# A transformer block on one core: the projections issued as 32-column matmuls behind the weighted sums

## What is computed

```python
x = x + _L0_attn_a_ref(_layernorm(x, axis=-1), ...)
x = x + _L0_ffn_ref(_layernorm(x, axis=-1), ...)
x = x + _L0_attn_b_ref(_layernorm(x, axis=-1), ...)
x = x + _L0_ffn_ref(_layernorm(x, axis=-1), ...)
```

## Time and profile before

| | |
|---|---|
| median of 3 runs | 992.39 us |
| span of the profiled execution | 987.4 us, 27821 instructions |
| the profiled execution's time around its span | not given apart; the median of the runs is 5.0 us above its span |
| TensorE matmuls | 917.8 us busy, 93% of the span |
| TensorE weight loads | 513.9 us, 52% |
| VectorE | 787.2 us, 80% |
| ScalarE | 772.6 us, 78% |
| GpSimd | 666.2 us, 67% |

### The profile page before, as it was taken

One profiled execution on the slowest core, in us unless ns is written; L12 is line 12 of the kernel. 1 busy time (PEld: TensorE's weight loads), 2 busy tenths in 40 slices (PEclk: granted clock), 3 DMA queues, 4 the chain that ended last, 5 costly groups with the idle time before them and its releaser, 6 DMA issues.

```text
span 987.4 us, 27821 instructions
## 1 busy us (share of the span) xinstructions
PE 917.8 (93%) x10286; PEld 513.9 (52%) x10286; DVE 787.2 (80%) x1394; ACT 772.6 (78%) x1299; POOL 666.2 (67%) x1280
## 2 busy tenths in 40 slices
PE   2589999999999999999999999999999998999885
PEld 1345555545555555555655555555555555654544
DVE  1688888898888888888788887888788878778524
ACT  2168888888888888888888888888888877887863
POOL 8465666667775886768676786768687585764442
PEclk9899999999999999999999999999999999999987
DMA  6577555444444443444444343444444454344001
GB/s 183 150 219 204 154 149 168 141 152 142 135 140 121 150 134 120 145 121 146 119 138 149 121 143 119 153 119 128 136 136 142 125 153 123 118 137 135 5 22 43
DMA packets 144694, 131.66 MB, mean 133 GB/s; under 512 B 9616, under 2 KB 127536, under 8 KB 144432
## 3 DMA queue, kind: packets, MB, share of 16 engines
q1 hardware_dynamic: 143456, 128.49, 43.8%
q10 hardware_dynamic: 1104, 1.41, 0.5%
HBM read 73.76 MB, written 55.57 MB: 131 GB/s over the span
## 4 chain that ended last, share of the span: by engine, by line
PE 67%; ACT 10%; DVE 9%; POOL 5%; issue 4%; DMA 3%; SPq 1%; POOLq 1%; ACTq 1%; DVEq 0%
PE values_bank L774 21%; PE ring L789 11%; PE ring L803 10%; PE m_bank L898 6%; DVE nmax L598 5%; PE m_bank L910 4%; PE m_bank L959 3%; PE m_bank L943 3%; PE m_bank L920 3%; ACT probs L669 2%; PE m_bank L931 2%; ACT hT L722 2%; ACT L713 2%; DMA k_stack<-scratch 2%; DMA scratch<-parts 1%
## 5 line engine op out<-in xcount | busy, mean ns | idle before, releaser
L598 DVE TENSOR_REDUCE nmax<-ring 128x4 f32<-128x1024 f32 x512 | 605.1, 1219 | 98.0 <-PE ring L789 97.0
L669 ACT ACTIVATE probs<-ring 128x1024 f32<-128x1024 f32 x512 | 518.2, 1025 | 54.8 <-PE ring L803 50.4
L774 PE MATMUL values_bank<-probs,values 128*32 128x256 f32 x4096 | 274.9, 386 | 0.7 <-ACT probs L669 0.6
L789 PE MATMUL ring<-k_stack,q_stack 64*128 64x256 bf16 x2048 | 201.2, 277 | 22.7 <-DMA k_stack<-scratch 18.6
L489 POOL TENSOR_SCALAR xy<-x,mv,rstd 128x128 f32<-128x128 f32 x256 | 200.6, 793 | 7.9
L803 PE MATMUL ring<-q_stack,k_stack 64*128 64x256 bf16 x2048 | 189.4, 273 | 8.5 <-DVE nmax L598 7.2
L774 PEld LDWEIGHTS values_bank<-probs,values 128*32 128x32 f32 x4096 | 107.1, 109 | 89.8 <-issue 37.2
L413 POOL TENSOR_SCALAR mparts<-nmax 128x32 bf16<-128x32 f32 x64 | 13.9, 217 | 188.0 <-DVE nmax L598 187.8
L789 PEld LDWEIGHTS ring<-k_stack,q_stack 64*128 64x128 bf16 x2048 | 70.3, 95 | 132.0 <-issue 56.0
L803 PEld LDWEIGHTS ring<-q_stack,k_stack 64*128 64x128 bf16 x2048 | 78.0, 94 | 93.9 <-issue 52.0
L511 POOL TENSOR_TENSOR parts<-rest,parts 128x512 bf16<-128x512 f32 x64 | 74.1, 1158 | 5.4
(11 more groups left out here) (102 smaller groups left out, 1084.0 us busy)
## 6 DMA issues: line engine op xcount, KB each, us to landing
q_stack<-scratch SPq DMA_DIRECT2D x128, 256.0 KB
k_stack<-scratch SPq DMA_DIRECT2D x128, 256.0 KB
scratch<-parts SPq DMA_DIRECT2D x128, 192.0 KB, 2.2
scratch<-parts SPq DMA_DIRECT2D x128, 128.0 KB, 2.2
scratch<-parts SPq DMA_DIRECT2D x128, 64.0 KB, 2.4
out<-x SPq DMA_DIRECT2D x16, 256.0 KB, 2.7
x<-in_x SPq DMA_DIRECT2D x3, 768.0 KB, 7.3
q_stack<-maxT SPq DMA_DIRECT2D x128, 12.0 KB
```

Of the source, the lines that this page charges most:

```text
L598: nc.vector.tensor_reduce(dst, src, axis=AX.X, op=ALU.max, negate=True).then_inc(max_done, 1)
L669: nc.scalar.activation(probs[g % 2][:, c:c + 2, :, :], pair_of("exps", n, p)[:, :, :].rearrange("p x (k q) -> p x k q", k=TILES), ACT.Exp) ...
L774: last = nc.tensor.matmul(values_bank[32 * c:32 * (c + 1), a * TOKENS:(a + 1) * TOKENS], values[turn % RING][:, k, PER_GROUP * g + c, :], ...
L789: last = nc.tensor.matmul(pair_of("scores", turn, p)[:, a, t * TOKENS:(t + 1) * TOKENS], q_stack[z][rows, p, t * P:(t + 1) * P], k_stack[z ...
```

## The change

A helper `by_columns` splits a projection's stationary tile into four pieces of 32 columns and issues one matmul for each, into the matching quarter of the output's partitions. qk, v and wo all go through it. TensorE's order in a step changes with it: qk goes directly behind w3, and E1, which stood ahead of S2, follows it; v goes from behind S4 to directly behind w1; wo goes directly behind w2, with E7 behind it instead of ahead; and E6 now stands ahead of xyT. On ScalarE the v copy moves from between exp3 and exp4 to between exp5 and the xyT copies; the oT2 copy stays between exp4 and exp5. `fill_m` is called in the new order: v now waits for oT2's reader, oT2 for on's, xyT for v's.

```diff
+QUADS, QUAD = 4, 32
...
+                    if p == 4 and live(n - 1):
+
+                        act.wait_ge(oT2_done, (n - 1) + 1)
...
-                    if p == 3 and live(n + 3):
+                    if p == 5 and live(n + 3):
 
                         act.wait_ge(v_done, (n + 3) + 1)
...
+                def by_columns(out, stationary, moving, start, stop):
+
+                    for c in range(QUADS):
+                        at = slice(QUAD * c, QUAD * (c + 1))
+                        last = nc.tensor.matmul(out[at], stationary[:, at], moving, start=start, stop=stop, skip_group_check=True)
+                    return last
...
                     if p == 1 and live(n - 1):
                         weigh(n - 1, 3)
-                    if p == 1 and live(n):
-                        exp_side(n, 1)
-                    if p == 2 and live(n + 4):
+                    if p == 1 and live(n + 4):
...
                         for a, wmat in enumerate((wq, wk)):
-                            last = nc.tensor.matmul(m_bank[:, a * TOKENS:(a + 1) * TOKENS], wmat, xnT[(n + 4) % 2][:, :],
-                                                    start=(a == 0), stop=(a == 1), skip_group_check=True)
+                            last = by_columns(m_bank[:, a * TOKENS:(a + 1) * TOKENS], wmat, xnT[(n + 4) % 2][:, :],
+                                              start=(a == 0), stop=(a == 1))
                         last.then_inc(qk_done, 1)
+                    if p == 1 and live(n):
+                        exp_side(n, 1)
...
-                    if p == 4 and live(n + 3):
-                        wv = projections[(n + 3) // ITEMS][2]
...
                     if p == 5 and live(n):
                         weigh(n, 1)
+                    if p == 5 and live(n + 3):
+                        wv = projections[(n + 3) // ITEMS][2]
+                        fill_m(pe, v_ready, (n + 3) + 1)
+                        for t in range(TILES):
+                            last = by_columns(m_bank[:, t * P:(t + 1) * P], xnT[(n + 3) % 2][:, t * P:(t + 1) * P], wv,
+                                              start=(t == 0), stop=(t == TILES - 1))
+                        last.then_inc(v_done, 1)
+                    if p == 6 and live(n):
+                        exp_side(n, 6)
...
-                    if p == 6 and live(n):
-                        exp_side(n, 6)
                     if p == 7 and live(n):
                         weigh(n, 2)
-                    if p == 7 and live(n):
-                        exp_side(n, 7)
...
                         for t in range(TILES):
-                            last = nc.tensor.matmul(m_bank[:, t * P:(t + 1) * P], onT[:, t * P:(t + 1) * P], wo,
-                                                    start=(t == 0), stop=(t == TILES - 1), skip_group_check=True)
+                            last = by_columns(m_bank[:, t * P:(t + 1) * P], onT[:, t * P:(t + 1) * P], wo,
+                                              start=(t == 0), stop=(t == TILES - 1))
                         last.then_inc(wo_done, 1)
+                    if p == 7 and live(n):
+                        exp_side(n, 7)
```

More of the change, by code:

```diff
@@ L724, in step @@
                             nc.scalar.activation(spare[:, len(BURSTS) + group:len(BURSTS) + group + 1], bqs[:, :], ACT.Exp)
-                    if p == 3 and live(n + 3):
+                    if p == 4 and live(n - 1):
+                        act.wait_ge(oT2_done, (n - 1) + 1)
+                        if n - 1 < ITEMS:
+                            last = nc.scalar.activation(onT[:, :], m_bank[:, 0:TOKENS], ACT.Identity, bias=wa[:, 514:515])
+                        else:
+                            last = nc.scalar.copy(onT[:, :], m_bank[:, 0:TOKENS])
+                        last.then_inc(onT_ready, 1)
+                    if p == 5 and live(n + 3):
                         act.wait_ge(v_done, (n + 3) + 1)
@@ L734, in step @@
                         last.then_inc(v_ready, 1)
[L735 to L742, removed]
                     if p == 5 and (live(n + 5) or live(n - 3)):
@@ L915, in step @@
                         down(group_at(n))
-                    if p == 4 and live(n + 3):
-                        wv = projections[(n + 3) // ITEMS][2]
-                        fill_m(pe, v_ready, (n + 3) + 1)
-                        for t in range(TILES):
-                            last = nc.tensor.matmul(m_bank[:, t * P:(t + 1) * P], xnT[(n + 3) % 2][:, t * P:(t + 1) * P], wv,
-                                                    start=(t == 0), stop=(t == TILES - 1), skip_group_check=True)
-                        last.then_inc(v_done, 1)
                     if p == 5 and live(n):
```

## The result

The changed kernel took 1065.33 us, the median of 4 runs (1064.18 to 1066.76), beside 992.49 us for the kernel before: a ratio of 1.0754, with a 95% interval of 1.0732 to 1.0776. It is 72.8 us slower. The profiled execution took 1066.21 us with a span of 1064.4 us, 77.0 more than the span before.

The account below looks back on a forecast made before the run. The prediction took round trips through ScalarE's exponentials and VectorE's maxima, not TensorE's own work, to bound the kernel. Longer ordinary and expert steps, less router savings, plus the last steps made 78.6 us: 992.4 + 78.6 = 1071 us, range 1050 to 1100.

Parts of the forecast that it names:

- The step: Ordinary step, E7 to E7: from 12.97 to 14.26 us in the first attention, 12.83 to 14.22 in the second.
- Price of the pieces: 32-column projections directly behind a weighted sum: 0.87 us for qk, 0.44 each for v and wo.
- rival of dear columns: Rival, 14%: 128-column pieces of v and wo cost 0.87 us each because issuing binds; 52 us more, up to 1121 us.
- What each move costs: Added per ordinary step: 0.44 us for wo behind w2, 0.58 for qk behind w3, 0.27 for v behind w1.
- Bound by TensorE's own work: Rival, 7%: work taken out of TensorE counts, 0.96 us a step, 58 us over 60 steps, giving 934 us.
- It doesn't do what it says: Case: a projection waits and no longer directly follows its weighted sum; 5 to 10 us, inside the range.
- The clock: Rival, 4%: TensorE's idle time lowers its granted clock to 0.95, some 36 us more, about 1107 us.
- Steps with experts: Each of 13 such steps takes 1.36 us more, with 0.27 given back at E5's wait; 17.7 us together.
- Router steps: qk covers E1's 0.49 us wait for VectorE: 0.5 us off each of 8 steps, -4 us together.
- The last steps: Last four steps, with fewer projections: 2 us added; steps with experts up to 59 counted at 1.36 us more each.
- The opening: Start of the program: it waits for DMA and does not change.
- what I put around the span: Time outside the profiled span: the median of the runs stands 5.0 us above the span, left as it is.

Follow-up runs that it names:

- E1: Not a run: a group of quads on TensorE in each step, whose result a ScalarE exponential reads; no time of its own.
- E7: Not a run: a later group of quads of the same kind in each step; ordinary steps are read from its start to its next start.
- E5: Not a run: a group of quads of the same kind in each step, which waits for VectorE's maxima in ordinary steps.

## Why the prediction was right

The forecast was 1071 us, the result 1065.33, by the mechanism that was named. Point by point:

- *The step.* 14.26 and 14.22 us were forecast for the two attentions, both came out at 14.25. E7 to S1 1.51 (1.51 forecast), S1 to w3 0.54 (0.54), w3 to E1 1.87 (1.87), E1 to S3 1.51 (1.51), S3 to on 0.76 (0.80), on to w0 0.59 (0.59), w0 to S4 1.00 (1.00), S4 to E5 1.72 (1.71), E5 to w1 0.32 (0.32), w1 to w2 2.99 (2.96), w2 to E7 1.44 (1.45).
- *Price of the pieces.* 0.87 for qk and 0.44 for v and wo: 1.87 less 1.00, and in w2 to E7 1.44 less 1.00. The rival of dear columns fell here. (Its price of 52 us makes 1123 with the 1071, not 1121; nothing hangs on it.)
- *What each move costs.* The forecast had wo at 0.44, qk at 0.87 - 0.19 - 0.10 = 0.58 and v at 0.51 - 0.24 = 0.27. Undone one at a time they gave back 0.41, 0.56 and 0.34. Of wo nearly the whole price was lost, because its old place had cost nothing; of qk and v a part.
- *Bound by TensorE's own work.* S1 begins 1.51 behind E7 and S3 1.51 behind E1, not 0.69 and 0.46. The pieces do take work out, but in these places it is worth 34 us of the rival's 58, against 106 for the order.
- *It doesn't do what it says.* qk waited for maxT in two steps of the opening, 1.1 us in all, and in no ordinary step; the pieces did follow the weighted sums.
- *The clock.* 1.00 in the middle, as forecast; the opening is told below.
- *Steps with experts.* 16.95 became 18.41, 1.46 more for 1.36. E5 no longer waits for exp4, but `up` (L838) now waits for the Gelu, 7.7 us in 13 times, because v no longer lies in between; with v behind S4 again that wait is 1.0 us in 6 times. That term was left out.
- *Router steps.* Five of them are steps with experts too, and took 1.07 to 1.18 more (17.61 to 18.68 in the first attention) where 1.36 - 0.5 was forecast. Step 11 has no experts and went from 14.01 to 14.25 where 1.29 - 0.5 was forecast: there the longer step covers not E1's 0.49 alone but all of the 1.04 by which the step was longer than an ordinary one.
- *The last steps.* 1.36 more was counted for each step with experts, but step 54 went from 20.03 to 18.45 and step 58 from 18.44 to 18.45. Before, mT waited there 1.46 and 1.37 us for GpSimd's `mparts`; the longer steps give GpSimd that time (with the pieces in the old places, and the short steps, it is 1.65 and 1.48 again). Step 55 went from 15.24 to 15.29; its E7 waited 1.76 us for VectorE before and 0.97 now, with wo ahead of it. Step 59, a router step too, went from 13.87 to 14.03.
- *The opening.* "Does not change" was wrong: step 0 went from 12.55 to 17.34 us.

In spans, steps 1 to 60 gave 70.2 us, step 0 4.8, the last part 2.1 and what lies ahead of step 0 -0.1, together 77.0 where 78.6 were forecast. Of the 5.7 us between forecast and median 1.6 are this; 3.2 are what I put around the span (5.0, where the profiled execution shows 1.8); 0.9 is the profiled execution against the median. That the sum came so near owes something to luck, misses of both signs in the special steps. Above their share of the forecast lie step 0 by 3.5 us, the ten steps with experts up to 51 by 2.1 and the end from step 60 on by 0.8; below it steps 54 to 59 by 5.7, the ordinary steps by 1.6 and step 11 by 0.55.

## What to carry to other kernels

Before moving work next to work of its own form, look at what it leaves: if it lay inside a round trip through another engine, its old place cost little or nothing, and the new one can cost up to its whole price (here 0.41 us of wo's 0.44, 0.56 of qk's 0.87, 0.34 of v's 0.44). List every reader of the shared buffers whose trip the move opens, not only the one that waits today. A saving on the busiest engine counts only where that engine's own work is what ends last.

## What was not expected of the hardware

**The clock in the opening.** Busy time by stretch, with the granted clock behind the engines, in the changed kernel:

```profile
53.00:60.00 7.00, 5.63 (x48) 2.58 (x50) 3.95 (x6) 3.03 (x5) 3.23 (x8) 0.50 0.69 201
60.00:66.00 6.00, 5.53 (x50) 2.11 (x50) 3.66 (x6) 3.98 (x4) 3.37 (x4) 0.50 0.76 227
66.00:72.00 6.00, 5.32 (x70) 2.53 (x62) 3.46 (x3) 3.14 (x6) 0.98 (x5) 0.80 0.49 137
```

And in the kernel before:

```profile
53.00:60.00 7.00, 6.72 (x61) 3.57 (x62) 5.43 (x7) 4.77 (x7) 4.67 (x10) 0.76 0.71 204
60.00:66.00 6.00, 5.17 (x72) 2.50 (x72) 4.64 (x6) 4.93 (x8) 2.59 (x6) 1.00 0.79 228
...
804.00:808.00 4.00, 3.86 (x28) 1.92 (x29) 1.31 (x2) 1.92 (x3) 3.73 (x6) 0.57 0.43 126
```

Behind a wait of 3.5 us or more for DMA, step 0 starts out at half the clock (1.2 GHz) in both, in the kernel before from its second quad on. Before, TensorE then worked almost without a gap and had the full 2.4 GHz from about 57 us; in the changed kernel, with gaps of 0.61, 0.69 and 0.47 us in step 0, it stayed at 1.2 GHz until about 68. A quad is listed with 0.61 us there and 0.39 behind it, a weighted sum with 1.93 and 1.07. In the stretch from 60 to 66 us the clock was 0.60 to 0.67 in three further runs with qk directly behind w3, and 1.00 in the two that put E1 ahead of qk. The late rise goes with the gaps; that they are its cause is not shown, since no run took the gaps alone away. The gaps of the middle of the run left it at 1.00. The last row is step 54 of the kernel before, behind the wait of 1.46 us for GpSimd: there too the clock fell for a few us, and a weighted sum took 1.94. Behind the 1.37 us of step 58 it stayed at 1.00, and with the pieces in the old places also behind a wait of 1.65 us in step 54 (1.00 from 802 to 806 us). So the length of the wait alone does not tell whether the clock falls.

**Pieces between quads are no dearer than whole projections.** Sixteen matmul records and sixteen weight loads of 32 columns took 0.58 us from start to start where four of 128 columns took 0.64.
